# Moving the scatters of a batch's third row block behind the root of the projection's normalisation

## The reference

```
x = x + layernorm(attention(layernorm(x)))      # 16 heads of 16, 4 key/value groups, rope, causal
x = x + layernorm(ffn(layernorm(x)))
ffn(x) = x + shared_mlp(x) + sum of 2 of 16 expert mlps, weighted by their normed sigmoid gates
mlp(x) = (silu(x @ wg) * (x @ wu)) @ wd         # 256 -> 128 -> 256
```

## Time and profile before

| what | value |
|---|---|
| time, median of 3 runs | 2366.59 us (2365.68 to 2369.12) |
| span of the profiled execution | 2472.9 us |
| the profiled execution's own time | none is given beside its span |
| busy in the span: PE, DVE, POOL, ACT | 93%, 78%, 69%, 57% |
| mean granted TensorE clock | 0.980 |

### The profile page before, as it was taken

One profiled execution on the slowest core, in us unless ns is written; L12 is line 12 of the kernel. 1 busy time (PEld: TensorE's weight loads), 2 busy tenths in 40 slices (PEclk: granted clock), 3 DMA queues, 4 the chain that ended last, 5 costly groups with the idle time before them and its releaser, 6 DMA issues.

```text
span 2472.9 us, 57907 instructions
## 1 busy us (share of the span) xinstructions
PE 2296.5 (93%) x17882; PEld 1478.5 (60%) x17882; DVE 1931.5 (78%) x5142; ACT 1399.3 (57%) x3208; POOL 1697.4 (69%) x2893
## 2 busy tenths in 40 slices
PE   5999999999999999999999999998789899999997
PEld 2565555555555555555555555554668787777754
DVE  6788888888888888888898888975455454677778
ACT  1565666656666566665666665665344454444444
POOL 4556777677776777777777767753656676777776
PEclk7999999999999999999999999998999999999999
DMA  4544445554455544445443444332344466788877
GB/s 133 136 140 147 144 133 156 155 165 138 138 155 146 165 137 142 133 138 157 122 132 111 141 137 129 113 100 70 114 142 146 136 190 201 250 278 283 273 257 253
DMA packets 289486, 391.76 MB, mean 158 GB/s; under 512 B 28000, under 2 KB 237920, under 8 KB 289056
## 3 DMA queue, kind: packets, MB, share of 16 engines
q1 hardware_dynamic: 263168, 316.72, 43.3%
q0 software_dynamic: 26016, 71.34, 7.9%
HBM read 186.84 MB, written 182.75 MB: 149 GB/s over the span
## 4 chain that ended last, share of the span: by engine, by line
PE 51%; POOL 26%; issue 8%; DVE 8%; ACT 3%; DMA 1%; another core or an unknown queue 1%; SPq 1%; POOLq 0%; ACTq 0%; DVEq 0%
PE bank L1710 9%; PE ps_a L859 6%; PE bank L1724 5%; PE ps_out L873 5%; PE ps_d L843 5%; PE ps_d L896 4%; POOL q_parts L683 4%; PE ps_d L889 4%; POOL sorted_dram L770 3%; PE bank L1691 3%; DVE roped_q L1124 3%; POOL rest L685 2%; POOL q_parts L685 2%; POOL guess L739 2%; PE ps_a L861 2%
## 5 line engine op out<-in xcount | busy, mean ns | idle before, releaser
L986 ACT ACTIVATE probs<-ps_a 128x512 f32<-128x512 f32 (+1 forms) x1408 | 713.1, 558 | 434.4 <-PE ps_a L861 339.4
L1109 DVE TENSOR_REDUCE negmax<-ps_d 128x2 f32<-128x768 f32 (+3 forms) x768 | 773.0, 1031 | 138.8 <-PE ps_d L845 73.8
L859 PE MATMUL ps_a<-qs,ks 99*128 99x512 bf16 (+3 forms) x2048 | 515.9, 302 | 19.2 <-ACT probs L986 15.6
L843 PE MATMUL ps_d<-ks,qs 96*128 96x128 bf16 (+3 forms) x2048 | 488.0, 304 | 22.1 <-DMA qs<-q_stack_dram 10.8
L845 PE MATMUL ps_d<-mask_max,ident_bf 128*128 128x128 bf16 x2048 | 394.9, 222 | 0.0
L861 PE MATMUL ps_a<-mask_exp,ident_bf 128*128 128x128 bf16 x2048 | 388.1, 220 | 0.0
L1621 POOL DMA_INDIRECT y_dram<-ysb,to_row x286 | 286.3, 1001 | 98.4 <-issue 53.5
L873 PE MATMUL ps_out<-probs,va 128*32 128x512 f32 (+3 forms) x4096 | 331.9, 442 | 4.1 <-DVE by_token L1159 4.1
L859 PEld LDWEIGHTS ps_a<-qs,ks 99*128 99x128 bf16 x2048 | 199.4, 98 | 202.7 <-ACT probs L986 66.6
L843 PEld LDWEIGHTS ps_d<-ks,qs 96*128 96x128 bf16 x2048 | 202.7, 99 | 191.1 <-DVE negmax L1109 40.6
L770 POOL DMA_INDIRECT sorted_dram<-h,slot x256 | 268.6, 1049 | 66.3 <-issue 65.4
(11 more groups left out here) (209 smaller groups left out, 4253.1 us busy)
## 6 DMA issues: line engine op xcount, KB each, us to landing
qs<-q_stack_dram SPq DMA_DIRECT2D x128, 384.0 KB
rows<-sorted_dram SPq DMA_DIRECT2D x286, 129.0 KB
y_in<-y_dram SPq DMA_DIRECT2D x32, 1024.0 KB
q_stack_dram<-q_parts SPq DMA_DIRECT2D x64, 384.0 KB, 3.0
x_in<-in_x SPq DMA_DIRECT2D x32, 512.0 KB, 4.3
q_stack_dram<-q_parts SPq DMA_DIRECT2D x64, 256.0 KB, 3.2
h_dram<-h SPq DMA_DIRECT2D x32, 512.0 KB
h<-h SPq DMA_DIRECT2D x32, 512.0 KB
```

Source lines behind the costliest of these rows:

```text
L843: pe.matmul(ps_d[:, number % 2, at:at + width], qs[0:KR, b % 2, h, j * P:(j + 1) * P], ks[0:KR, b % 2, g, 0:width], start=True, stop=False)
L859: pe.matmul(ps_a[:, number % 3, at:at + width], ks[0:KM, b % 2, g, j * P:(j + 1) * P], qs[0:KM, b % 2, g * HG + h0 + k, j * P:T], start=Tr ...
L986: act.activation(probs[:, at:at + nh * width], ps_a[:, number % 3, 0:nh * width], ACT.Exp) \
L1109: dve.tensor_reduce(negmax[:, g // 2, j, at:at + nh], src, AX_X, ALU.max, negate=True) \
```

## The change

`scatter2`, the two scatters of row block j = 2, is issued at slot (1,4) instead of (0,10). Slots are walked by each engine in order, so on GpSimd the two indirect DMAs now stand behind `root_proj` (1,2) and ahead of `split0a` (1,5). They stay ahead of `scatter3`. In turns in which `root_proj`, the split or `root_1` don't exist, the slot moves in the same way. No other engine reads this entry, and the counts on the semaphores are the same.

```
-    "scatter2": (0, 10),
+    "scatter2": (1, 4),
```

## The result

The changed kernel takes 2430.09 us (median of 4 runs, 2425.70 to 2432.09) against 2366.14 (4 runs, 2365.51 to 2369.12): ratio 1.0271, 95% interval 1.0259 to 1.0283. It is slower by 64 us, where 57 was forecast.

What follows compares the result with a forecast made beforehand. The prediction took a loop through GpSimd's section up to `root_1` as the bound. 26 x 2.34 = 60.8, plus 0.8, less 2.5, gave 59.1 us, scaled to 56.6: 2366.6 + 56.6 = 2423 us, range 2388 to 2445.

Steps and rivals of the forecast that it cites:

- The mechanism: On GpSimd behind `root_proj`, the pair delays the first split and `root_1` by 2.34 us, all of it entering each lap.
- The two side terms: Around VectorE's residual add: up to 0.49 us back at `scatter3`, up to 0.82 us lost by GpSimd's split, per turn.
- The 0.49 us at `scatter3`: On GpSimd, the second instruction of `scatter3`, moved clear of the residual add, takes 0.96 us instead of 1.45.
- rival 3: GpSimd's first split collides with the residual add, losing 0.82 us a turn, with nothing regained at `scatter3`: 2443 us; chance 0.12.
- The sum: Whole kernel: turns 3 to 28 add 60.8 us, turn 2 0.8, turn 31 gives back 2.5; together 59.1 us.
- scaling with 0.957: Whole kernel: the profiled sum of 59.1 us, scaled evenly to the shorter timed runs, becomes 56.6 us.
- The gain of 0 ahead of `root_proj`: On GpSimd, removing the pair there gains 0: idle time grows to 5.17 us, as VectorE's moments release the root.
- a lap of 54.3 us: In turns 3 to 28 of the profile after, each lap should take 54.3 us instead of 51.99.
- New idle time of ScalarE ahead of the `LN2` normalisation: On ScalarE in turns 3 to 28, up to 2.3 us, or else a wait for `root_1` above 2.24 us.
- rival 4: An earlier `root_proj` on GpSimd pays in every turn as in turn 31, 0.5 us each: 2354 us; chance 0.03.
- Rival 1: TensorE bounds the timed kernel; GpSimd's loop has room from 2.34 us a turn, hiding the delay: 2364 to 2367; chance 0.08.
- rival 2: Half the delay drowns in about 1.2 us of room a turn in GpSimd's loop: 2394 us; chance 0.15.

Runs made afterwards that it cites:

- second profile of before: The kernel before, run once more with no edit: 2367.21 us, ratio 1.0007, with a profile span of 2363.5 us.
- half a pair: The kernel before with only the second of the two `scatter2` scatters moved behind `root_proj`, to (1,4): 2398.90 us, ratio 1.0139.
- before, shorter roots: The kernel before with the Newton step left out of each root on GpSimd: 2346.49 us, ratio 0.9918.
- changed, shorter roots: The changed kernel with the Newton step left out of each root on GpSimd: 2346.40 us, ratio 0.9921 to before.
- `root_1` moved: `root_1` put ahead of two split stages on GpSimd: from before 2383.81 us, ratio 1.0076; from the changed kernel 2428.29 us, ratio 1.0266 to before.

## Why the prediction was right

**The mechanism** was right: a pair of scatters put on GpSimd between `root_proj` and the first split makes everything behind it late, and goes into each lap. The lap can be cut at three points: the end of `root_proj`'s moments on VectorE, the start of the first split, and the end of `root_1`. The moments, in turn 13 of the second profile of before and in turn 12 of the changed kernel:

```profile
734.11 0.28 DVE L1091 BATCH_NORM_AGGREGATE moments<-stats 128x2 f32<-128x6 f32 x3
708.74 0.28 DVE L1091 BATCH_NORM_AGGREGATE moments<-stats 128x2 f32<-128x6 f32 x3
```

The three sections in turn 12 of six kernels, from their traces:

| kernel | moments to first split | to the end of `root_1` | to the next moments |
|---|---|---|---|
| before, second profile | 3.60 | 24.65 | 21.3 |
| half a pair | 4.53 | 24.99 | 21.3 |
| changed | 5.79 | 24.79 | 21.3 |
| `scatter2` behind the first split | 3.60 | 27.20 | 21.3 |
| before, shorter roots | 3.59 | 22.71 | 23.0 |
| changed, shorter roots | 4.66 | 22.94 | 21.7 |

The third section is that of the other engines. In all the kernels with GpSimd time added it is 21.3 us, so that is its length when nothing is spare in it, and before has the same: it has no room. Where GpSimd's time is taken away the third section grows, and that is the room. From before to the changed kernel the first section grew by 2.19 us and the second by 0.14; together 2.33, where I had 2.34. So close a hit is in part luck: the first split waited 0.48 us in the timed kernel and not 0.20, so the pair itself cost 2.19, and the rest came from `scatter3`, where I had expected a gain.

**The two side terms** were set off against each other, and that held because neither is there in its size. The 0.49 us at `scatter3` were in the first profile alone: its second scatter took 1.45 us there, 0.99 in the second profile and 0.96 in the changed kernel, while its first now took 1.25 instead of 1.09. The first split, 1.28 us, lost nothing beside the residual add; VectorE lost 1.05 us there, all in the first of the two adds (1.73 instead of 0.68 us), which began 0.11 us behind the split. The rule quoted from the Trainium skill, "SBUF — State Buffer", section "Who interferes with whom", was borne out on VectorE's side (2.33 against 1.28 us), and rival 3, which let it cost GpSimd 0.82 us a turn, was not.

**The sum.** Turns 3 to 28 gave 26 x 2.32 = 60.3 us, where I had 60.8. The first split of turn 3 is 5.3 us later (248.03 - 242.69): 2.3 of them are its own pair, and 0.8 are there at the first split of turn 1, before any scatter, so turn 2 cost 2.2, where I had 0.8; the 1.68 us of idle time that I took off is 0.09 us in the second profile. Turn 29 cost nothing in the end and turn 31 gave back 2.5, both as I had it: behind turn 31's root the changed kernel is 60.3 us later (1686.24 - 1625.90). From there to the end it loses another 4, where I had nothing. I have not followed these; behind the first split of turn 29 the two kernels with shorter roots differ by 6 us in their profiles as well. Together 64.3, the difference of the two spans (2427.8 - 2363.5), and of the medians, 64.0. I had 59.1, and made it 56.6 by scaling with 0.957. That scaling was the wrong step: it took the profiled execution for an evenly stretched one, while the durations of GpSimd's instructions are nearly all the same in both profiles (0.96, 0.20, 1.27; the 1.45 us above is an exception), and what differs is the waits between the engines.

**What was right for the wrong reason.** The gain of 0 ahead of `root_proj` rested on 2.66 us of idle time that the timed kernel does not have. It held because even with 0.3 us to spare the moments, not the scatters, release the root. In the changed kernel the idle time is 3.03 us, 0.3 plus the pair and 0.2, where I said 5.2; and "a lap of 54.3 us" was wrong in the same way. New idle time of ScalarE ahead of the `LN2` normalisation, which I put at up to 2.3 us, was 0.7. The difference of the laps was right, their level was not. In turn 31, on which rival 4 rested, the second profile has the order of the first (root 3.24 us behind its moments, 1625.90 against 1622.66), and in the changed kernel it is 0.71 us (1686.24 against 1685.53): the 2.5 us were given back there. Of the other turns only turn 2 had anything to give, 0.4 us.

**The rivals.** Rival 1 started from the right remark, that the timed lap must be about 49.7 us (it is 49.54), and drew from it that GpSimd might then have room. It has none: half a pair costs 1.28 us a lap, which rules out rival 2 as well. What I could not see from one profile is that TensorE and the rest, at 49.33, and GpSimd's loop, at 49.54, are nearly tied. The chain of waits shows only the one that wins: in the second profile it gives GpSimd 5% (over the whole span), in the first 26%, of the same kernel.

**What stays open.** Why the first profiled execution was 109 us longer. In its laps TensorE stood still 1.5 us ahead of the second q projection and ScalarE waited some 2.6 us for something the trace has no name for; none of the other eleven profiles has these waits. I did not see it recur, and the second profile shows that the kernel runs without it. Nor did I separate, in the changed kernel, how much travels through `root_1` and how much through `root_2`: `root_1` moved alone changes nothing, `root_2` was never moved alone, and the last experiment, which gave the time back, shortened all three roots.

## What to carry to other kernels

An instruction that sits in front of a wait is covered only as far as that wait is long; behind the wait it costs all of its time, if what follows is the loop that sets the lap. Test such a claim with a filler of about the same length in the new place and with work taken away: the first showed here that time and not transfers was the price, the second that the place stops mattering once the engine has 3 us less to do. And when a profile's span is several per cent off the timed median, take another profile before reading idle times from it: sums of durations survived here, but for one scatter, while the idle time ahead of `root_proj` was 2.66 us in one profile and 0.31 in the other. When two kernels differ in time, look at the granted clock lap by lap too, or what it costs passes for something else.

## What the runs showed of the hardware

- The power operation on GpSimd takes 1.04 us for 128x4 elements, where an add of that size takes 0.20 (709.54 to 711.66 for two, with the gap between them). Leaving the Newton steps out of the three roots of a lap takes some 3 us of GpSimd's time away, and before gets 0.8% faster.
- VectorE's small operations are not safe from GpSimd's: the addition on 128x4 elements of L1186 takes 0.15 us in the mean in the changed kernel with shorter roots, 0.45 in the second profile of before and 0.68 with `root_1` moved; the cast of 128x8 in L1188 takes 0.17 in the first two, 0.55 in the third, and 1.06 in the changed kernel with `root_1` moved, where in turn 12 it ends (748.79) just behind the k split's last stage on GpSimd (748.76).
- With `scatter2` at (1,6) TensorE stood still for 1.7 us in each lap, and in nine of 26 laps its granted clock fell to 1.2 GHz for 3.4 us shortly behind that; such a lap is 0.75 us longer. In before and in the changed kernel, whose laps lack this stand-still, it was 1.00 throughout turns 3 to 28.
- An indirect scatter of 128 rows occupies GpSimd for 0.96 us at least, wherever it stood, and for 1.25 to 1.46 in single places: the first of `scatter3` behind the late first split (1.25 in the changed kernel, 1.46 with half a pair) and the second in the first profile of before (1.45).
